# A recommender's interaction layers on one core: the sum over eight partial sums, cut into four column slices

## The reference, cut to what matters

```
def _cin_layer(X0, Xi, W, b):
    Wr = W.reshape(H, F0_, Fi)
    return einsum('hjk,bjd,bkd->bhd', Wr, X0, Xi) + b[None, :, None]
Xi = X0
for W, b in Ws:                     # three layers, H = 128
    Xi = _cin_layer(X0, Xi, W, b)
    res.append(Xi.sum(axis=2))
z = concatenate(res, axis=1)
h = maximum(concatenate([z, dense_ctx], 1) @ W_top1 + b_top1, 0)
h = maximum(h @ W_top2 + b_top2, 0)
y = h @ W_top3
```

## Time and profile before

| | us |
|---|---|
| median of 3 runs | 725.35 |
| lowest, highest | 723.96, 726.55 |
| the profiled execution's own time | 724.48 |
| its span, first to last instruction | 722.5 |
| TensorE busy in it | 657.1 (91%) |
| VectorE busy | 574.4 (79%) |
| GpSimd busy | 442.1 (61%) |
| ScalarE busy | 414.9 (57%) |

### The profile page before, as it was taken

How to read it: one execution, slowest core, us unless ns; L and a number is a source line. 1 busy time by engine, 2 the same in 40 slices (tenths; PEclk the granted TensorE clock), 3 DMA queues, 4 the chain that set the end, 5 groups by cost and what they waited for, 6 DMA issues and landing times.

```text
span 722.5 us, 10598 instructions
## 1 busy us (share of the span) xinstructions
PE 657.1 (91%) x2856; PEld 490.3 (68%) x2856; DVE 574.4 (79%) x1495; ACT 414.9 (57%) x1369; POOL 442.1 (61%) x372
## 2 busy tenths in 40 slices
PE   0079999999999999999999999999999999999998
PEld 0047676777678776767678767676768877676667
DVE  5049898989894798999995598999997589998870
ACT  3025666666662666657663466766664475666651
POOL 6737777777773477786865358686765366344440
PEclk9999999999999999999999999999999999999999
DMA  6247404040403003021211202213030300300000
GB/s 206 66 137 261 122 11 119 6 120 4 121 6 109 16 3 117 10 86 40 75 52 49 74 4 61 66 31 96 18 109 17 95 16 18 105 2 5 0 2 1
DMA packets 39055, 44.33 MB, mean 61 GB/s; under 512 B 17427, under 2 KB 22253, under 8 KB 38867
## 3 DMA queue, kind: packets, MB, share of 16 engines
q1 hardware_dynamic: 33363, 42.34, 19.3%
q0 software_dynamic: 5632, 1.31, 2.0%
HBM read 8.86 MB, written 0.00 MB: 12 GB/s over the span
## 4 chain that ended last, share of the span: by engine, by line
PE 71%; DVE 15%; issue 4%; POOL 4%; ACT 3%; DMA 2%; SPq 1%; POOLq 0%; DVEq 0%
PE p_u L535 16%; PE p_u L537 15%; PE p_u L536 15%; PE p_x L519 12%; DVE parts L450 8%; DVE x2t L458 5%; PE p_z L554 5%; PE p_g L545 4%; POOL emb L258 3%; DVE z L421 2%; ACT x1f L308 1%; ACT x1h L313 1%; PE p_z L581 1%; PE p_h L567 1%; PE p_h L566 1%
## 5 line engine op out<-in xcount | busy, mean ns | idle before, releaser
L332 ACT ACTIVATE prod<-p_u,x0t 128x128 f32<-128x128 f32 x1024 | 291.9, 369 | 151.6 <-PE p_u L537 151.2
L535 PE MATMUL p_u<-w1h,x1h 128*128 128x512 f32 (+1 forms) x640 | 307.3, 480 | 25.7 <-DVE parts L450 23.4
L450 DVE SCALAR_TENSOR_TENSOR parts<-p_u,x0t,parts 128x128 f32<-128x128 f32 x1024 | 284.0, 343 | 56.1 <-PE p_u L537 54.3
L537 PE MATMUL p_u<-w1h,x1l 128*128 128x512 f32 (+1 forms) x640 | 250.2, 391 | 0.0
L536 PE MATMUL p_u<-w1l,x1h 128*128 128x512 f32 (+1 forms) x640 | 249.7, 390 | 0.0
L258 POOL DMA_INDIRECT emb<-table_in,idx_all x176 | 190.1, 1080 | 51.2 <-issue 47.1
L274 POOL TENSOR_TENSOR parts<-parts,prod 128x512 f32<-128x512 f32 x128 | 169.2, 1322 | 71.3 <-ACT prod L332 59.6
L535 PEld LDWEIGHTS p_u<-w1h,x1h 128*128 128x128 f32 x640 | 120.6, 188 | 84.6 <-DVE parts L450 48.6
L269 POOL TENSOR_TENSOR parts<-prod 128x512 f32<-128x512 f32 x64 | 82.7, 1292 | 135.4 <-ACT prod L332 134.8
L536 PEld LDWEIGHTS p_u<-w1l,x1h 128*128 128x128 f32 x640 | 121.4, 190 | 42.9 <-issue 20.2
L537 PEld LDWEIGHTS p_u<-w1h,x1l 128*128 128x128 f32 x640 | 120.6, 189 | 26.2
(11 more groups left out here) (37 smaller groups left out, 180.0 us busy)
## 6 DMA issues: line engine op xcount, KB each, us to landing
fac_b<-xx SPq DMA_DIRECT2D x96, 234.0 KB
fac_a<-xx SPq DMA_DIRECT2D x48, 78.0 KB
emb<-table_in,idx_all POOLq DMA_INDIRECT x176, 2.7
g_all<-w_in SPq DMA_DIRECT2D x3, 832.0 KB, 9.4
xx<-xx SPq DMA_DIRECT2D x32, 78.0 KB
fac_b<-xx SPq DMA_DIRECT2D x16, 156.0 KB
w<-w_in SPq DMA_DIRECT2D x1, 2496.0 KB, 9.9
bd<-x0t SPq DMA_DIRECT2D x128, 10.0 KB, 1.9
```

What stands on the lines that cost most here:

```text
L332: last = nc.scalar.activation(dst[:, i * H:(i + 1) * H], u[:, i * H:(i + 1) * H], ACT.Copy, scale=x0t[:, par, t, j:j + 1])
L450: nc.vector.scalar_tensor_tensor(out=chain[:, p, i, :], in0=u[:, i * H:(i + 1) * H], scalar=x0t[:, par, t, j:j + 1], in1=add, op0=ALU.mult ...
L535: nc.tensor.matmul(u, xh, wh, start=True, stop=False)
L537: nc.tensor.matmul(u, xl, wh, start=False, stop=True).then_inc(u_full, 1)
```

## The change

The one reduction of a tile, 128 columns out of 8 x 128, becomes four reductions of 32 columns out of 8 x 32. They stand in front of the chains of quads 3, 5, 7 and 9 of the next tile. Only the first of them carries waits: for all chains of its tile, all three GpSimd additions of its tile, and `layer2` of two tiles before. `x2_made` now counts four per tile, and who waits for it waits for four times the number. Behind the last tile all four run one behind the other.

```
-Q_X2 = 7
+Q_X2 = (3, 5, 7, 9)
+X2_PARTS = len(Q_X2)
...
-                    need(pool, x2_made, T - 1)
+                    need(pool, x2_made, X2_PARTS * (T - 1))
...
-            def fold_x2(T, p):
-                dve.wait_ge(chained, CHAIN_TILE * (T + 1))
-                dve.wait_ge(summed, SUM_TILE * (T + 1))
-                need(dve, g_full, T - 1)
-                nc.vector.tensor_reduce(out=x2t[:, p, :], in_=parts[:, p].rearrange("p a h -> p h a"),
+            def fold_x2(T, p, i):
+
+                if i == 0:
+                    dve.wait_ge(chained, CHAIN_TILE * (T + 1))
+                    dve.wait_ge(summed, SUM_TILE * (T + 1))
+                    need(dve, g_full, T - 1)
+                h = slice(i * H // X2_PARTS, (i + 1) * H // X2_PARTS)
+                nc.vector.tensor_reduce(out=x2t[:, p, h], in_=parts[:, p, :, h].rearrange("p a h -> p h a"),
                                         op=ALU.add, axis=AX.X).then_inc(x2_made, 1)
...
-                        if q == Q_X2 and (has_prev or tt > 0):
-                            fold_x2(T - 1, (tt + 1) % 2)
+                        if q in Q_X2 and (has_prev or tt > 0):
+                            fold_x2(T - 1, (tt + 1) % 2, Q_X2.index(q))
...
-            fold_x2(T, T % 2)
+            for i in range(X2_PARTS):
+                fold_x2(T, T % 2, i)
...
-                pe.wait_ge(x2_made, T + 1)
+                pe.wait_ge(x2_made, X2_PARTS * (T + 1))
```

More of the change, by code:

```diff
@@ L441, in chain_quad @@
                     dve.wait_ge(a_scaled, A_TILE * T + 1)
-                    need(dve, x2_made, T - 1)
+                    need(dve, x2_made, X2_PARTS * (T - 1))
                 u = p_u[(QUADS * tt + q) % RING]
```

## The result

The changed kernel takes 707.3 us (median of 4 runs, 705.89 to 709.09) against 724.9: a ratio of 0.9744, interval 0.9718 to 0.9769, so 2.6% faster by the ratio; the medians lie 17.6 us apart. The profiled execution took 705.89, its span is 703.9, 18.6 less than before. The forecast was 702.6 with a range of 692 to 714.5.

What follows compares the result with a forecast made beforehand. TensorE was taken as the bound, with VectorE nearly one too. Stalls removed save 31.4 us, less 9.3 for a new stall and 0.2 in the last macro: 21.9 off 724.48 gives 702.6 us, range 692 to 714.5.

Steps and rivals of the forecast that it cites:

- The bound and the stalls removed: TensorE is the bound; its waits for late VectorE chains go, 31.4 us saved in all.
- stall A: TensorE's wait at quad 3 of a macro's last tile: 0.78 us, 12 times, 9.4 us, forecast to go.
- stall B: TensorE's wait at quad 1 of the next macro, after the seam: 1.17 us, 15 times, 17.6 us, forecast to go.
- the small waits ahead of A: TensorE's wait at quad 1 of a macro's last tile: 0.09 us, 12 times, 1.1 us, forecast to go.
- those between the tiles of the last macro: TensorE's stall in each tile where nothing is prepared: 1.1 us each, 3.3 us saved but for 0.2.
- The price of a slice: A 32-column reduction on VectorE takes 0.53 us (bounds 0.48 to 0.80); four take 2.12 against 1.93 for the whole.
- the second rival's case: The errata's fixed cost of 151 cycles per VectorE instruction holds, so a slice takes 0.6 us.
- What comes late next: After each seam product 1 waits about 0.5 us for GpSimd; quad 9 stalls 0.62, 15 times, 9.3 us lost.
- The start: One more TensorE stall, before the first reduction, stays as it is.
- Rival 1: Product 4 meets GpSimd's third addition; quad 3 of the next tile stalls 0.81: 9.3 us more, 712; chance 0.30.
- Rival 2: No collision that matters at the seam, product 1 slips in ahead of the addition: all 31.4 saved, 693; chance 0.13.
- Rival 3: VectorE becomes the bound with slices of 0.80 us: 25 us slower, 750; chance 0.07.

Runs made afterwards that it cites:

- the short additions: GpSimd's three additions each cover 16 of 512 columns: in the changed kernel 703.35 us, ratio 0.9639; in the kernel before 727.7 us, ratio 0.9973.
- the moved product: The changed kernel with product 1 at slot 3 instead of 5: 700.5 us, ratio 0.9600; again on another chip 694.7 us, ratio 0.9558.

## Why the prediction was right

The measured 705.89 of the profiled execution is 3.3 above the forecast, and the median of 707.3 lies in the range, but just above the narrower 699 to 706 that the forecast itself was given.

*The bound and the stalls removed.* Right, with one cause missing: stall A was put down to the reduction alone, and the short additions show that the collision of product 6 was as necessary to it. (The first macro begins a block and has a stall A all the same, the one of the earlier trace rows; the last macro has none, and the count of 12 holds.) Stalls A and B and the small waits ahead of A are gone from every macro, and those between the tiles of the last macro too; the stretch behind the last macro's first transposes fell from 93.99 to 89.74 us.

*The price of a slice.* 0.53 forecast, 0.49 to 0.54 in the timeline, mostly 0.51. With the other sizes the line is complete: 0.29 for 16 columns (half a pair), 0.52 for 32, 0.98 for 64, 1.89 for 128, which is 0.06 + 1.8 ns for each element read. The fixed cost of 151 cycles in the Trainium skill ("VectorE: DVE Perf Modes", section on the TRN2 errata; an estimate of 0.16 us) is not in any of these four start spacings. The rival that such a cost would have made is the prediction's first; where its text says "the second rival's case", it means that one.

*What comes late next.* The step was right in kind and place: product 1 meets GpSimd's first addition, and quad 9 of the first tile waits. Its size was too small. It was put at 0.62; by the starts of TensorE it is 0.70 of gap and 0.11 behind it, 0.81. Counted from the end of the last `add_group` (1.59 before `x1l`'s start at 119.85), the chain of quad 5 ends at +13.14 instead of +13.0 and TensorE stands ready at +12.57 instead of +12.6: small differences of a difference. In 12 macros that is 12 x 0.19 = 2.3 us. One had it worse: at 331.93 the idle column has 1.05, since product 1 (328.86, 1.98 long) waited out the whole addition; 0.7 more than forecast. In the second macro the same 0.80 comes in two parts, at quads 5 and 9. Its count was off by one: there are 14 such places and not 15, for the last macro makes no products; 0.6 less.

*The start.* It was taken as unchanged, and in this execution it was 1.1 us later (first transposes of the second macro at 49.87 instead of 48.78); it differs from execution to execution. In the profiled executions of the other kernels, on several chips, it came between 48.36 and 55.66 (later still with the clearing of the short additions), a spread larger than the whole error of the forecast; that it was only 1.1 here is luck.

The account: 21.9 forecast, less 2.3, 0.7 and 1.1, and 0.6 more for the missing place, make 18.4. The spans differ by 18.6. The four sizes that were off are small and mostly of one sign, so the forecast did not come out by errors that cancel.

*Rival 1,* a second collision with product 4, did not happen: that product is 0.72 long at 141.87 and comes just ahead of GpSimd's third addition, whose row with the second takes 3.00 from 140.76 instead of 2.7. *Rival 2's* 693 is what the moved product gives (0.9600 and 0.9558 of 724.9 are 696 and 693): the collision costs 10.4 to 13.5 us by the ratios, from different chips, and 14 x 0.79 = 11 by the macros, where 9.3 was reckoned. *Rival 3* fell with the price of a slice. The first slice never waited for GpSimd.

*Where the reasoning was incomplete.* The text had the reason for stall B (two slices fall into VectorE's wait for `x1h`) but did not ask whether the place would do without the cut. The runs take this apart. The place alone, with no cut, gives 1.14 of the 1.28 us a macro. The cut is worth more than the 0.14 between them, but only once product 1 is out of the way (36.7 against 35.9); in the changed kernel a collision takes most of it back.

## What to carry to other kernels

Look where the engine idles before cutting its work: a long instruction that falls into a wait is nearly free there (37.98 to 36.84 us a macro by its place alone), and the same one behind the wait holds up a bank. Cutting pays where the pieces must go between deadlines that are closer together than the whole is long, and here costs 0.06 us apiece. And after any move, compare start times of the instructions that can block each other on two engines; moving one product two slots earlier, or one later, was worth more than half of the change itself.

## What the runs showed of the hardware

- A VectorE product of two SBUF operands and a GpSimd addition did not overlap in any row read here. The one that comes second waits out the first: products took up to 1.98 instead of 0.68, additions 1.90 instead of 1.29, and with additions of 16 columns no product took over 0.70. Within about 0.1 us of each other either can be first (129.04 against 128.97 went to VectorE; 328.86 against 328.98 to GpSimd), so such a place can differ from macro to macro.
- VectorE's reductions are not touched by GpSimd: the slices of the changed kernel are 0.57 to 0.62 long throughout, whatever GpSimd does.
- The granted TensorE clock stood at half (1.2 GHz instead of 2.4) for 3.4 to 10.4 us at the start of every profiled execution. In nine of the fourteen it did so again in the tail, and in seven inside a network macro, where TensorE had run the network's 128 x 128 matmuls just before. One such stretch (3.6 us from 390.6) made a network macro 1.6 us longer (53.85 against 52.25 within the execution with product 1 at slot 3). Runs of the changed kernel ran from 705.89 at 0.995 to 709.09 at 0.988 mean clock, so their spread of 3 us may be this alone.
